# Down projection: four of eleven groups in two passes on bare 4-bit values, scaled afterwards

## What is computed

```python
h = _layernorm(x) * (1 + cb) + sb
w_gu   = dequant_fp4(gate_up_packed, gate_up_scales, 128)   # 2*1408 x 512
w_down = dequant_fp4(down_packed, down_scales, 128)         # 512 x 1408
gate, up = split(h @ w_gu.T)
m = silu(gate) * up
y = m @ w_down.T            # y[t, o] = sum_g scale[g, o] * (sum_{i in g} m[t, i] * val[o, i])
y = y / sqrt(mean(y * y, axis=-1) + 1e-6)
x = x + gb * y
```

## Time and profile before

| | us |
|---|---|
| median of 3 runs | 2078.53 |
| lowest, highest | 2077.65, 2078.73 |
| the profiled execution | 2079.21 |
| its span, first to last instruction | 2077.4 |
| TensorE busy in the span | 2053.1 (99%) |
| VectorE busy | 1330.6 (64%) |
| ScalarE busy | 1050.1 (51%) |
| GpSimd busy | 720.8 (35%) |

### The profile page before, as it was taken

One profiled execution on the slowest core, in us unless ns is written; L12 is line 12 of the kernel. 1 busy time (PEld: TensorE's weight loads), 2 busy tenths in 40 slices (PEclk: granted clock), 3 DMA queues, 4 the chain that ended last, 5 costly groups with the idle time before them and its releaser, 6 DMA issues. The chain is left out here.

```text
span 2077.4 us, 36904 instructions
## 1 busy us (share of the span) xinstructions
PE 2053.1 (99%) x12073; PEld 1806.6 (87%) x12073; DVE 1330.6 (64%) x3060; ACT 1050.1 (51%) x1963; POOL 720.8 (35%) x540
## 2 busy tenths in 40 slices
PE   9999999999999999999999999999999999999998
PEld 7888899999999999999999999999997788788787
DVE  6453567676675766757667565565655777799643
ACT  4422455555555555555555555555554333688622
POOL 2030436254372543725427000000017455488400
PEclk9999999999999999999999999999999999999999
DMA  7885321212212122121221201201034667011421
GB/s 253 240 247 183 94 73 56 88 51 65 73 50 89 50 66 75 45 89 50 71 75 41 76 23 53 60 26 53 25 101 135 247 219 239 32 40 41 142 71 61
DMA packets 174444, 195.78 MB, mean 94 GB/s; under 512 B 13731, under 2 KB 119587, under 8 KB 174115
## 3 DMA queue, kind: packets, MB, share of 16 engines
q1 hardware_dynamic: 172067, 190.66, 29.5%
q10 hardware_dynamic: 2304, 4.20, 0.5%
HBM read 124.41 MB, written 70.39 MB: 94 GB/s over the span
## 5 line engine op out<-in xcount | busy, mean ns | idle before, releaser
L1219 ACT ACTIVATE pT_hi<-ps_t 128x512 fp32r<-128x512 f32 (+3 forms) x640 | 304.0, 535 | 246.2 <-PE ps_t L1145 244.0
L1304 DVE TENSOR_TENSOR pT_lo<-ps_t,pT_hi 128x512 fp32r<-128x512 f32 (+3 forms) x640 | 356.2, 604 | 57.2 <-ACT pT_hi L1219 55.7
L1227 ACT ACTIVATE probs<-probs,rmin 128x128 f32<-128x128 f32 (+15 forms) x256 | 309.3, 1210 | 163.7 <-DVE rmin L1295 163.3
L207 PE MATMUL ps_z<-pT_lo,v_hi 128*128 128x256 f32 (+1 forms) x1152 | 325.0, 282 | 0.0
L208 PE MATMUL ps_z<-pT_hi,v_lo 128*128 128x256 f32 (+1 forms) x1152 | 324.8, 282 | 0.0
L206 PE MATMUL ps_z<-pT_hi,v_hi 128*128 128x256 f32 (+1 forms) x1152 | 317.9, 276 | 3.0 <-DVE pT_lo L1304 3.0
L1145 PE MATMUL ps_t<-ident,probs 128*128 128x128 f32 x2176 | 283.5, 273 | 0.1
L1145 PEld LDWEIGHTS ps_t<-ident,probs 128*128 128x128 f32 x2176 | 245.4, 140 | 9.3 <-ACT probs L1227 0.5
L206 PE MATMUL ps_s<-kq 128*128 128x512 f32 (+3 forms) x640 | 247.1, 386 | 2.4 <-PEq L354 1.1
L208 PE MATMUL ps_s<-kq 128*128 128x512 f32 (+3 forms) x640 | 231.1, 361 | 0.0
L207 PE MATMUL ps_s<-kq 128*128 128x512 f32 (+3 forms) x640 | 230.5, 360 | 0.0
(11 more groups left out here) (198 smaller groups left out, 4215.0 us busy)
## 6 DMA issues: line engine op xcount, KB each, us to landing
scratch_v<-p_vo_hi SPq DMA_DIRECT2D x64, 256.0 KB, 2.9
scratch_v<-p_x SPq DMA_DIRECT2D x64, 256.0 KB, 3.4
v_hi<-scratch_v SPq DMA_DIRECT2D x64, 256.0 KB, 3.4
v_lo<-scratch_v SPq DMA_DIRECT2D x64, 256.0 KB, 4.0
scratch_zT<-z SPq DMA_DIRECT2D x256, 64.0 KB, 1.7
w_raw<-in_w_qkv SPq DMA_DIRECT2D x16, 512.0 KB, 3.8
tile_z<-scratch_zT SPq DMA_DIRECT2D x14, 512.0 KB, 6.5
tile_scales<-scratch_recips SPq DMA_DIRECT2D x14, 512.0 KB, 8.3
```

Source lines behind the costliest of these rows:

```text
L207: nc.tensor.matmul(dst, stat[0], mov[1], start=False, stop=False)
L1219: nc.scalar.activation(pT[0][:, slot, i % 2, 0:w], ps_t[:, (chunks_before(i) + u) % T_BANKS, 0:w], ACT.Copy).then_inc(t_hi, 1)
L1227: nc.scalar.activation(probs[:, i % 2, 0:w], probs[:, i % 2, 0:w], ACT.Exp, bias=rmin[:, i % 2:i % 2 + 1], scale=-1.0, accum_out=sums[:, i ...
L1304: nc.vector.tensor_tensor(pT[1][:, slot, i % 2, 0:w], ps_t[:, (chunks_before(i) + u) % T_BANKS, 0:w], pT[0][:, slot, i % 2, 0:w].bitcast(F ...
```

## The change

Groups 0 to 3 (`BARE = 4`) of the down projection are treated as gate-up is: the weights are bare values, TensorE takes two passes a group into a PSUM bank of its own, and the scales go on behind it. Groups 4 to 10 stay as they are, three passes each into `ps_y`.

- In attention the decoder still multiplies by `qscale`, but reads it from a scratch array `dscales` whose rows 0 to 3 hold 1.0 (GpSimd sets four rows with a memset, SyncE writes the array with two DMAs).
- `factors` holds the scales of groups 0 to 3, sent to all 128 partitions (16-bit; three in a new tile, one in `gate_a`, which is free by then). For groups 0 to 3 only the hi part of `wdn` is loaded.
- TensorE, each tile: 4 x 2 + 7 x 3 = 29 matmuls. Six PSUM banks serve the bare groups, four a tile; `bank_freed` says which product must be over before a bank is written again.
- VectorE: `scale_term` (four products a tile, PSUM x factors into `terms`), `join` (ps_y + terms[0] into `raw`), `mean` and `scale_y` (now from `raw`). `terms` has one buffer for each of the four groups, `raw` has one buffer. What finishes tile t - 1 stands between the products of tile t.
- GpSimd: `add_term` three times a tile (terms[0] += terms[n]) and `add_x` (y += x1), which VectorE did.
- ScalarE: the square reads `raw`, and `mid_hi` of the next tile comes behind it.

The diff, cut to what the text speaks of:

```diff
+BARE = 4
@@ attention, SyncE
-                sp.dma_start(qscale[:, :], dn_scales[bass.ds(h, 1), :].to_broadcast([P, D])) \
+                if is_at(h, 0):
+                    sp.wait_ge(dscales_saved, 2 * 16)
+                sp.dma_start(qscale[:, :], hbm["dscales"][bass.ds(h, 1), :].to_broadcast([P, D])) \
...
+                sp.dma_start(hbm["dscales"][BARE:NI, :], dn_scales[BARE:NI, :]).then_inc(dscales_saved, 16)
+                sp.wait_ge(units_ready, 1)
+                sp.dma_start(hbm["dscales"][0:BARE, :], qscale[0:BARE, :]).then_inc(dscales_saved, 16)
@@ attention, GpSimd
+        nc.gpsimd.memset(qscale[0:BARE, :], 1.0).then_inc(units_ready, 1)
@@ gate_up_and_down, SyncE
+        for n in range(BARE):
+            sp.dma_start(factors[n], dn_scales[n:n + 1, :].to_broadcast([P, D])).then_inc(factors_loaded, 16)
...
-                for k in range(2):
+                for k in range(wd_parts(n)):
@@ TensorE
-            else:
-                pe.wait_ge(y_done, t - 1)
             pe.wait_ge(m_lo, t + 1)
-            for n in range(NI):
+            for n in range(BARE):
...
+                wait_for(pe, term_ready, bank_freed(tile, n))
+                hi, lo = [part[:, n, :] for part in ms[parity]]
+                nc.tensor.matmul(bare_bank(parity, n), hi, wd(0, n), start=True, stop=False)
+                nc.tensor.matmul(bare_bank(parity, n), lo, wd(0, n), start=False, stop=True).then_inc(bare_ready, 1)
...
+            elif not (isinstance(t, int) and t < 2):
+                pe.wait_ge(raw_ready, t - 1)
+            for n in range(BARE, NI):
@@ VectorE
+        def scale_term(tile, n):
+            dve.wait_ge(bare_ready, BARE * tile.t + n + 1)
+            if n == 0:
+                wait_for(dve, raw_ready, tile.t)
+            nc.vector.tensor_tensor(terms[:, n, :], bare_bank(tile.parity, n), factors[n], ALU.mult).then_inc(term_ready, 1)
+
+        def join(tile):
+
+            dve.wait_ge(sum_step, SUMS * (tile.t + 1))
+            dve.wait_ge(y_ready, tile.t + 1)
+            wait_for(dve, y_scaled, tile.t)
+            nc.vector.tensor_tensor(raw[:, :], ps_y[tile.parity], terms[:, 0, :], ALU.add).then_inc(raw_ready, 1)
...
+                join(tile.before())
+            for n in range(2):
+                scale_term(tile, n)
+            if not first:
+                mean(tile.before())
+            scale_term(tile, 2)
+            if not first:
+                scale_y(tile.before())
+            for n in range(3, BARE):
+                scale_term(tile, n)
             if not last:
                 mid_lo(tile.after())
@@ GpSimd
+        def add_term(tile, n):
+            pool.wait_ge(term_ready, BARE * tile.t + n + 1)
+            wait_for(pool, sum_step, SUMS * tile.t + n - 1)
+            nc.gpsimd.tensor_tensor(terms[:, 0, :], terms[:, 0, :], terms[:, n, :], ALU.add).then_inc(sum_step, 1)
...
+            for n in range(1, BARE - 1):
+                add_term(tile, n)
+            if not first:
+                add_x(tile.before())
+            add_term(tile, BARE - 1)
```

More of the change, by code:

```diff
@@ L1612, in gate_up_and_down @@
     sg = sb("g_silu", [P, 2, BT], F32)
+    factor_rows = sb("d_factors", [P, BARE - 1, D], F16)
+    factors = [factor_rows[:, n, :] for n in range(BARE - 1)] + [gate_a[:, 0:D // 2].bitcast(F16)]
+    until_down.close()
+    terms = ph.enter_context(nc.sbuf_tensor("d_terms", [P, BARE, D], F32, side="right"))
     ps = ph.enter_context(nc.psum_tensor("g_ps", [P, 2, DC, BT], F32))
@@ L1630, in gate_up_and_down, with bare_bank, bank_freed @@
     out_saved = [sem(f"out_saved{n}") for n in range(2)]
-    ps_y = [ps[:, 0, n, :] for n in range(2)]
-    Y_STEPS = 2
+    ps_y = [ps[:, 1, n, :] for n in range(2)]
+    room = [ps[:, 0, n, :] for n in range(DC)] + [ps[:, 1, n, :] for n in range(2, DC)]
+    ROOM_OF = ((0, 1, 2, 3), (4, 5, 0, 1))
+    SUMS = BARE - 1
+    def bare_bank(parity, n):
+        return room[ROOM_OF[parity][n]]
+    def bank_freed(tile, n):
+        at = ROOM_OF[tile.parity][n]
+        other = ROOM_OF[1 - tile.parity]
+        back, index = (1, other.index(at)) if at in other else (2, n)
+        if isinstance(tile.t, int) and tile.t < back:
+            return 0
+        return BARE * (tile.t - back) + index + 1
     block = ph.enter_context(nc.Block())
@@ L1755, in _, with finish, step @@
         act.wait_ge(mid_ready, NI * NB)
[L1757 to L1765, removed]
+        def finish(tile):
+            act.wait_ge(raw_ready, tile.t + 1)
+            nc.scalar.activation(junk[:, :], raw[:, :], ACT.Square, accum_out=ss[:, :]).then_inc(square_ready, 1)
             act.wait_ge(mean_ready, tile.t + 1)
             nc.scalar.activation(rms[:, :], ms_eps[:, :], ACT.Sqrt).then_inc(rms_ready, 1)
+        def step(tile, first, last):
+            if not first:
+                finish(tile.before())
+            if not last:
+                mid_hi(tile.after())
         token_tiles(act, step)
+        finish(LAST)
     @block.vector
@@ new lines, in mean, with scale_y @@
+        def mean(tile):
+            dve.wait_ge(square_ready, tile.t + 1)
+            nc.vector.tensor_scalar(ms_eps[:, :], ss[:, :], 1.0 / D, RMS_EPS, ALU.mult, ALU.add) \
+              .then_inc(mean_ready, 1)
+        def scale_y(tile):
+            t, parity, k = tile
+            dve.wait_ge(rms_ready, t + 1)
+            nc.vector.reciprocal(rrms[:, :], rms[:, :]).then_inc(dve_step, 1)
+            dve.wait_ge(dve_step, t + 1)
+            wait_for(dve, out_saved[parity], 16 * k)
+            nc.vector.scalar_tensor_tensor(out=y[:, parity, :], in0=raw[:, :], scalar=rrms[:, 0:1],
+                                           in1=gate_b[:, :], op0=ALU.mult, op1=ALU.mult).then_inc(y_scaled, 1)
@@ L1814, in step @@
                 mid_lo(tile.after())
[L1815 to L1823, removed]
@@ L1824, in step @@
-            dve.wait_ge(dve_step, Y_STEPS * t + 2)
-            dve.wait_ge(x1_loaded[parity], 16 * (k + 1))
-            nc.vector.tensor_tensor(y[:, parity, :], y[:, parity, :], x1[:, parity, :], ALU.add).then_inc(y_done, 1)
-        token_tiles(dve, step)
+        token_tiles(dve, step)
+        join(LAST)
+        mean(LAST)
+        scale_y(LAST)
+        dve.wait_ge(y_scaled, NT)
+        dve.wait_ge(x1_loaded[LAST.parity], 16 * (LAST.k + 1))
+        nc.vector.tensor_tensor(y[:, LAST.parity, :], y[:, LAST.parity, :], x1[:, LAST.parity, :], ALU.add).then_inc(y_done, 1)
```

40 lines of the change are left out of this document (33 added, 7 removed).

## The result

| | before | changed |
|---|---|---|
| median, us | 2078.63 (4 runs) | 2102.41 (4 runs) |
| lowest, highest | 2077.65, 2079.98 | 2101.32, 2103.04 |
| span of the profiled execution | 2077.4 | 2099.5 |
| ratio changed to before | | 1.0111, 95% interval 1.0099 to 1.0123 |

The change makes the kernel 1.1% slower, 23.8 us, though TensorE has 64 matmuls less. The page's first part, before and then changed, shows that the work went where it was meant to go: TensorE has 64 instructions less, VectorE 65 and GpSimd 64 more.

The account below looks back on a forecast made before the run. TensorE alone bound the down projection; afterwards a VectorE-GpSimd ring would. First join 1959.2, 14 periods of 9.4, a step of 8.0 and tail 6.0 give span 2104.8; plus 1.8, less 0.7: 2105.9 us, range 2095 to 2115.

Parts of the forecast that it names:

- period: Down projection, time from one tile's join to the next: 7.56 us undisturbed plus 1.87 of waiting, 9.4 us.
- tail from the last join: End of the kernel: the join's 0.72 us ahead of the 5.3 us of before, 6.0 us together.
- The bound before: Down projection before the change: TensorE alone binds, 33 matmuls a tile at 0.2333 us, 7.70 us a tile.
- The ring: Down projection: join, products 0 and 1, GpSimd's four adds, next join wait on each other in a loop; 7.56 us undisturbed.
- The prices: VectorE's product and join in the down projection: 0.68 us each, from the nearest row; bounds 0.60 and 0.75.
- The turns: Down projection: GpSimd adds and VectorE instructions with two SBUF operands wait for each other, 0.46 and 1.41, together 1.87 us a tile.
- TensorE's idle time: Down projection, ahead of each tile's first matmul: TensorE waits 2.6 us for `mid_lo`, busy some 72% of the stage.
- The start: Start of the down projection: last product of gate-up at 1951.69 as before, TensorE's first tile at 1948.62, first join at 1959.2.
- Rival A: Down projection: VectorE and GpSimd take no turns, 7.56 us a tile, 2078.3 us, no change; 4 in 100.
- rival B: Down projection: TensorE keeps the pace at 6.77 us a tile, 2064.3 us, faster; 3 in 100.
- Rival C: Down projection: TensorE's clock falls after idle times; if it stayed low, 12.4 us a tile, 2149 and some; 4 in 100.
- What costs nothing: Memset and two DMA issues at attention's start, four factor loads before the last weight loads: nothing, or 1 us without cover.

Follow-up runs that it names:

- the runs on the scaling and on `mid_lo`: Each against the changed kernel: scaling of y reads PSUM instead of `raw`, 2097.92 us; `mid_lo` of the next tile moved right behind the join, 2104.2 us.

## Why the prediction was right

Forecast 2105.9 us in a range of 2095 to 2115, slower; measured 2102.4. Against the span I had summed (2104.8; measured 2099.5) the terms stand like this:

| step of the sum | predicted | measured |
|---|---|---|
| last product of gate-up starts | 1951.69 | 1950.74 |
| first join | 1959.2 | 1958.09 |
| join and two products until add 1 starts | 2.2 | 2.25 |
| GpSimd's four at 1.29, undisturbed | 5.16 | 5.16 |
| handovers within and behind them | 0.2 | 0.03 |
| add 2 held up by the scaling of y | 0.46 | 0.32 |
| add of x held up by `mid_lo` | 1.41 | 1.38 |
| period | 9.4 | 9.14 |
| step without `mid_lo` | 8.0 | 7.61 |
| tail from the last join | 6.0 | 6.07 |

Measured are the rows of the timeline above. The undisturbed length is 1.29, as add 3 has it; what add 2 (1.61) and the add of x (2.67) have over it is the holding up; the handovers are the sum of gaps and overlaps between the rows.

- *The bound before*, TensorE at 0.2333 us a matmul, was read rightly; that its passes would be worth nothing afterwards was shown by the run with the third pass.
- *The ring.* The step that carried the forecast, that one buffer and the order of the adds set the period, held: moving one add off the ring took 1.24 us out of the period.
- *The prices.* Product and join were 0.68 to 0.69 us as taken from the nearest row; the 16-bit factor costs nothing that shows. From the product's end to add 1, with the register instruction between, it is 0.16 us, where I had 0.2.
- *The turns* held, and were mis-sized by 0.17: the scaling of y is held up by what is left of add 1 (it comes 0.7 us before its end, as estimated), and add 2 lost 0.32, not 0.46. The turn itself is as long as at 107.56: in both places the scaling ends 0.55 us behind the add that it waited for. But there the next add starts 0.04 us before that add ends, and here 0.08 behind it, so that some 0.12 less of the wait falls into its row. The sum counted this piece twice, in the 0.46 and in the 0.1 between add 1 and add 2.
- *The period* was too long by 0.26, or 0.29 before rounding (the terms add up to 9.43): 0.17 from the turns and 0.17 from handovers, which I took at 0.1 each and which are 0.08 between add 1 and add 2 and 0.03 from add 3 to the join, with small overlaps between the other rows, less 0.05 for the part ahead of add 1, where product 0 starts 0.80 behind the join's start and not 0.72. The joins are 9.12 apart on average; over 14 periods this is 3.9 us of the error of 5.3 in the span, the earlier first join 1.1, the last step 0.4, less 0.1 for the tail. The difference in the median is only 3.5, and that is luck: I took the median to lie 0.7 below the profiled execution, and it lies 1.1 above.
- *TensorE's idle time* ahead of a tile was put at 2.6 us and is 2.11 where the clock stayed up: the period is shorter, and the step behind a tile's first matmul (0.34) and the row of its last (0.39) are longer than the 0.233 that the sum had for each. Its busy share of the stage, put at 72%, is 82% from 1960 to 2080 us, tiles at the low clock included.
- *The start* of the stage is not as fixed as the sum took it. GpSimd's last add of gate-up ends between 1946.7 and 1953.1 us in the eleven profiles (before, changed, and nine of the kernels above), though nearly nothing differs up to there. A sum to 1 us cannot be had from one profile; the period can.
- *Rival A* (no turns) fell with the runs on the scaling and on `mid_lo`, *rival B* (TensorE keeps the pace) with the first timeline, and needed other kernels to come true. *Rival C* happened in its harmless form, below. *What costs nothing*, the memset, the DMAs at the start of attention and the factor loads, cannot be told from the drift of the start, so that their price is not shown; attention's first scores start at 216.7 us in the changed kernel and 217.9 before.

## What to carry to other kernels

When work is taken off the bound engine and given to others, draw the ring of waits that the new work closes, buffer by buffer, and add up its length: with one buffer, its length is the period, though no engine on it is near full (here VectorE is busy for 72% and GpSimd for 74% of 1960 to 2080 us, their waits for a turn counted). Then look at every instruction with two SBUF operands on VectorE: beside an add of GpSimd one of the two waits, here for up to 1.39 of the 1.61 us of `mid_lo`, and it pays to put it where GpSimd is idle, or to read one operand from PSUM. And the number of pieces moved is a dial: here three of eleven, with the order mended, bring 0.5%, four in the order given cost 1.1%.

## What the runs showed of the hardware

TensorE's granted clock fell five times in the down projection of the changed kernel, each time in a tile ahead of which TensorE had been idle for 2.1 or 2.2 us, and in five of the nine such tiles. Busy time and clock (0.50, 1.00 and 0.50) of two of the falls and the stretch between them:

```profile
1993.00:1996.30 3.30, 3.30 (x9) 2.63 (x8) 1.76 (x3) 0.72 (x2) 1.41 (x2) 0.50 0.49 159
1996.40:2020.20 23.80, 19.03 (x80) 14.44 (x79) 17.69 (x25) 5.92 (x10) 18.72 (x11) 1.00 0.14 44
2020.30:2023.60 3.30, 3.30 (x10) 2.54 (x9) 1.65 (x3) 0.72 (x2) 1.51 (x2) 0.50 0.38 127
```

0.50 is the 1.2 GHz level. The tile of a fall takes 1.6 us longer and its successor starts after 0.54 us of idle time instead of 2.11 (2001.30 in the timeline above), so the ring never noticed: up to that of tile 14 the joins stay 9.03 to 9.17 us apart. With idle times of 1.20 us (the third pass put back) the clock was 1.00 over the whole stage. The Trainium skill ("TensorE: Matmul & The Clock Gate", A second HAM failure mode: psum-queue depth-cycling) describes such a swing for short idles between groups of matmuls; the trace shows it behind idle times of 2.1 us and not behind those of 1.20, and shows no cost as long as TensorE has slack.

The turn goes to whoever comes first, however small the margin. In the kernel with the second buffer the same two instructions, `mid_lo` and the add of x, fell one way in one tile (2002.29 and 2002.04, the add first by 0.25 us) and the other way in the next (2010.53 and 2010.56, `mid_lo` first by 0.03), and the period differed by 0.6 us between them.
